# Five layer norms with the reciprocal deviations spread by two 16-bit matmuls, written out by half images

## Chip, cores and metric

The kernel runs on one core of one Trainium2 chip. The metric is the device time of one execution in microseconds (us). TensorE does the matmuls (PE in the profile's rows; PEld is its loading of weights), VectorE is DVE, ScalarE is ACT, GpSimd is POOL. SBUF is the on-chip memory that all of them read, PSUM the memory that matmuls write.

## The reference, cut to what matters

A feature map of 8 images, 128 channels and 32 x 32 pixels goes through a window attention, a gated depthwise convolution, and then, as 1024 tokens of 128 channels per image, through full attention, a mixture of gelu experts, a local attention and a mixture of silu experts. Every token stage begins with a layer norm over the channels, and the local attention ends with a fifth that has a gain and an offset:

```python
def _ln_t(v, eps=1e-05):
    m = jnp.mean(v, axis=-1, keepdims=True)
    s = jnp.var(v, axis=-1, keepdims=True)
    return (v - m) / jnp.sqrt(s + eps)

t = t + _L2_attn_ref(_ln_t(t), ...)
t = t + _L2_ffn_ref(_ln_t(t), ...)
t = t + _L3_attn_ref(_ln_t(t), gamma, beta)   # ends with (out - mu) * rsqrt(var + EPS) * gamma + beta
t = t + _L3_ffn_ref(_ln_t(t), ...)
```

## The kernel before

The whole network is one program of stages, one behind the other; each stage ends with a barrier of all engines (`Chip.stage`, L68 to L76). `network` calls `layer_norm` (L1425) five times: ahead of the token attention (L2300), ahead of the gelu experts (L2313, weights are fetched meanwhile), ahead of the local attention (L2317), behind it (L2321, the one with gain and offset, called the fourth below), and ahead of the silu experts (L2329, again with a fetch). Nothing else runs in these stages.

The map X lies in SBUF with the 128 channels on the partitions, so a mean over channels is a sum over partitions, which TensorE makes. The work is cut into 16 halves of images, 512 tokens each. For a half there are these steps, all in float32 unless said otherwise:

- mean (L1465, TensorE): one matmul with a matrix whose entries are 1/128 leaves the mean of each token on all partitions, 128 x 512 in PSUM (`m_ps`);
- centre (L1513, VectorE): `xc` = X minus `m_ps`;
- Square (L1495, ScalarE): `sq`;
- variance (L1473, TensorE): four matmuls with `sq` as weights and one column of 1/128, so that the 512 variances come out as a tile of 128 x 4 (`v_ps`), tokens on the partitions;
- Sqrt (L1500, ScalarE) and reciprocal (L1519, VectorE), both on 128 x 4: `sd` and `rs`;
- broadcast (L1483, TensorE): four matmuls of 128 x 128 with a column of `rs`, repeated, as weights and the unit matrix as data put each token's reciprocal deviation back on all partitions, 128 x 512 in PSUM (`r_ps`);
- finish: XN = `xc` times `r_ps` (L1523, VectorE), or in the fourth norm t = `xc` times gamma times `r_ps` (L1526) and X = t + beta + X (L1530).

The order on each engine is written out by hand in pairs of halves (an image), in a hardware loop that `periods` (L1446) makes: the front of an image (two means, two centres) stands ahead of the back of the image before it (on VectorE two reciprocals and two finishes, on TensorE two variances and two broadcasts). Semaphores tie the engines together. GpSimd has no instruction in these stages.

Of the kernel before, what the change touches and what calls it, by code (L numbers as in the profile page):

```python
# [47 lines left out]
LO = 2.0 ** 11  # L48
# [1376 lines left out]
def layer_norm(chip, src, mean_w, eps5, identf, dst=None, X=None, gamma=None, beta=None, fetch=None):  # L1425

    nc = chip.nc
    TILES = HALF // C
    with chip.stage() as ctx:
        xc = chip.buf(ctx, "xc", [C, 2, 2, HALF])
        sq, t = (chip.buf(ctx, n, [C, 2, HALF]) for n in ("sq", "t"))
        sd, rs = (chip.buf(ctx, n, [C, 2, TILES]) for n in ("sd", "rs"))
        scratch = chip.buf(ctx, "scratch", [1, 8])
        m_ps, v_ps, r_ps = (chip.psum(ctx, n, [C, 2, HALF]) for n in ("m_ps", "v_ps", "r_ps"))
        mean_ready, centred, squared, var_ready, rooted, inverted, spread, scaled, stored = (chip.sem(s) for s in (
            "mean_ready", "centred", "squared", "var_ready", "rooted", "inverted", "spread", "scaled", "stored"))  # L1440

        def periods(engine, front, back):


            front(0, 0)
            with engine.Fori(0, B // 2 - 1) as i:  # L1446
                for odd in (1, 0):
                    front(i * 2 + (2 - odd), odd)
                    back(i * 2 + (1 - odd), 1 - odd)
            front(B - 1, 1)  # L1450
            back(B - 2, 0)
            back(B - 1, 1)

        with nc.Block() as block:
            if fetch is not None:
                @block.sync
                def _(sp):
                    fetch.load(sp)

            @block.tensor  # L1460
            def _(pe):
                def front(i, odd):
                    for c in range(2):
                        pe.wait_ge(centred, i * 2 + c + 1)
                        nc.tensor.matmul(m_ps[:, c], mean_w[:], src[:, i, c * HALF:(c + 1) * HALF],  # L1465
                                         start=True, stop=True).then_inc(mean_ready, 1)

                def middle(i):
                    for c in range(2):
                        pe.wait_ge(squared, i * 2 + c + 1)  # L1470
                        pe.wait_ge(rooted, i * 2 + c + 1)
                        for n in range(TILES):
                            mm = nc.tensor.matmul(v_ps[:, c, n:n + 1], sq[:, c, n * C:(n + 1) * C], mean_w[:, 0:1],  # L1473
                                                  start=True, stop=True)
                        mm.then_inc(var_ready, 1)

                def back(i, odd):
                    middle(i)
                    for c in range(2):
                        pe.wait_ge(inverted, i * 2 + c + 1)  # L1480
                        pe.wait_ge(scaled, i * 2 + c + 3)
                        for n in range(TILES):
                            mm = nc.tensor.matmul(r_ps[:, c, n * C:(n + 1) * C],  # L1483
                                                  rs[:, c, n:n + 1].to_broadcast([C, C]), identf[:], start=True, stop=True)
                        mm.then_inc(spread, 1)

                periods(pe, front, back)

            @block.scalar
            def _(act):  # L1490
                def front(i, odd):
                    for c in range(2):
                        act.wait_ge(centred, i * 2 + c + 3)
                        act.wait_ge(var_ready, i * 2 + c + 1)
                        nc.scalar.activation(sq[:, c], xc[:, odd, c], ACT.Square).then_inc(squared, 1)  # L1495

                def back(i, odd):
                    for c in range(2):
                        act.wait_ge(var_ready, i * 2 + c + 3)
                        nc.scalar.activation(sd[:, c], v_ps[:, c, 0:TILES], ACT.Sqrt, bias=eps5[:]).then_inc(rooted, 1)  # L1500

                with act.Fori(0, B // 2) as i:
                    for odd in range(2):
                        front(i * 2 + odd, odd)
                        back(i * 2 + odd, odd)

            @block.vector
            def _(v):
                def front(i, odd):
                    for c in range(2):  # L1510
                        v.wait_ge(mean_ready, i * 2 + c + 1)
                        v.wait_ge(scaled, i * 2 + c + 1)
                        nc.vector.tensor_tensor(xc[:, odd, c], src[:, i, c * HALF:(c + 1) * HALF], m_ps[:, c],  # L1513
                                                ALU.subtract).then_inc(centred, 1)

                def back(i, odd):
                    for c in range(2):
                        v.wait_ge(rooted, i * 2 + c + 3)
                        nc.vector.reciprocal(rs[:, c], sd[:, c]).then_inc(inverted, 1)  # L1519
                    for c in range(2):  # L1520
                        v.wait_ge(spread, i * 2 + c + 1)
                        if dst is not None:
                            nc.vector.tensor_tensor(dst[:, i, c * HALF:(c + 1) * HALF], xc[:, odd, c], r_ps[:, c],  # L1523
                                                    ALU.mult).then_inc(scaled, 1)
                            continue
                        nc.vector.scalar_tensor_tensor(t[:, c], xc[:, odd, c], gamma[:], r_ps[:, c],  # L1526
                                                       ALU.mult, ALU.mult).then_inc(scaled, 1)
                        v.wait_ge(scaled, i * 2 + c + 5)
                        at = X[:, i, c * HALF:(c + 1) * HALF]
                        nc.vector.scalar_tensor_tensor(at, t[:, c], beta[:], at, ALU.add, ALU.add).then_inc(stored, 1)  # L1530

                grant(nc, scratch, [(centred, 2), (rooted, 2), (var_ready, 2), (scaled, 4)])
                periods(v, front, back)


def token_projections(chip, XN, dram, qk_scr, v_scr):
# [586 lines left out]
def local_attention(chip, XN, dram, identf, out):  # L2123
# [131 lines left out]
def network(nc, x, dram, out):  # L2255
# [12 lines left out]
    with ExitStack() as ctx:  # L2268
# [143 lines left out]
```

## Time and profile before

| | us |
|---|---|
| median of three runs | 3694.21 |
| the three runs | 3693.68, 3694.21, 3706.76 |
| the profiled execution, its own time | 3697.97 |
| its span (first to last instruction in the trace) | 3696.2 |
| the five layer norms' stretches together | 237.6 |

Over the whole span the page has TensorE busy 88%, VectorE 74%, ScalarE 57% and GpSimd 31%; most of that is attention and experts. The norms are some 6.4% of the span, so they have to be read by themselves: by the busy times of a stretch, by the instructions in order of time, and by the mean durations of a line. A bracket at a row's end says how long the engine was idle ahead of it and what ended that. A group that repeats (x16) is given with its start and the length to its last end, which overlaps the next group's start by some 0.1 to 0.2 us on TensorE, since its ends are modelled. PEclk is the share of TensorE's full clock that was granted: 1.00 is 2.4 GHz and 0.50 is 1.2 GHz.

### The profile page before, as it was taken

The numbers are of one execution on the slowest core, as the hardware profiler recorded it, in microseconds if no ns is written. First come the engines' busy times: TensorE is split into PE (matmuls) and PEld (weight loads), VectorE is DVE, ScalarE is ACT, GpSimd is POOL, SyncE is SP. The second block draws the span as 40 slices with busy tenths as digits, with TensorE's granted clock in tenths as the row PEclk, the third lists the DMA queues.
The fourth block names the chain that finished last, engine by engine and source line by source line (L and its number), as shares of the span: only waits on it lengthen the run. The fifth ranks groups of instructions, "written<-read, shape, count | busy, mean of one in ns | idle before, by whom it ended". The sixth has DMA issues, their size and how long they took to land. (4 is left out here: it accounts for less than half of the span.)

```text
span 3696.2 us, 77563 instructions
## 1 busy us (share of the span) xinstructions
PE 3265.0 (88%) x29519; PEld 1473.0 (40%) x29519; DVE 2743.4 (74%) x4441; ACT 2106.7 (57%) x2679; POOL 1139.6 (31%) x990
## 2 busy tenths in 40 slices
PE   5978887467799999999999999779978959999999
PEld 3545554134222222222222222633466724444444
DVE  6468885564799999999999995244377467777776
ACT  2338887012277777787778778334333335555555
POOL 4515656000000000000000000034300168888887
PEclk9979999788699999999999999779988779999999
DMA  5756664003200010001000000034300133233320
GB/s 158 209 142 137 139 145 88 4 0 139 70 17 23 17 28 17 23 17 28 23 17 24 22 18 5 19 114 152 103 1 0 47 103 102 92 85 100 90 85 29
DMA packets 133923, 243.65 MB, mean 66 GB/s; under 512 B 34984, under 2 KB 47440, under 8 KB 133136
## 3 DMA queue, kind: packets, MB, share of 16 engines
q1 hardware_dynamic: 125968, 221.96, 21.5%
q0 software_dynamic: 7680, 17.84, 2.1%
q8 instruction: 195, 3.19, 0.4%
q14 instruction: 80, 0.66, 0.1%
HBM read 167.36 MB, written 56.62 MB: 61 GB/s over the span
## 5 line engine op out<-in xcount | busy, mean ns | idle before, releaser
L1170 DVE TENSOR_REDUCE mxv<-mx_ps 128x1 f32<-128x512 f32 x2048 | 1255.4, 681 | 58.2 <-PE mx_ps L1024 57.7
L1145 ACT ACTIVATE PT<-st_ps 128x1024 f32<-128x1024 f32 x1024 | 998.3, 1021 | 267.5 <-PE st_ps L1037 262.8
L1054 PE MATMUL o_ps<-PT,VA 128*32 128x256 f32 x8192 | 655.6, 392 | 3.8 <-ACT OR L1129 1.2
L2119 POOL TENSOR_TENSOR hg<-u,gb 128x512 f32<-128x512 f32 x352 | 580.4, 1654 | 130.2 <-DVE u L2080 99.9
L1024 PE MATMUL mx_ps<-KS,QS 24*128 24x512 f16 x2048 | 581.5, 393 | 35.8 <-DVE mxv L1170 19.2
L1037 PE MATMUL st_ps<-QS,KS 26*128 26x512 f16 x2048 | 398.5, 386 | 0.0
L2080 DVE TENSOR_TENSOR u<-h_ps,s 128x512 f32<-128x512 f32 x352 | 242.9, 690 | 189.3 <-ACT s L2041 185.0
L2041 ACT ACTIVATE s<-h_ps 128x512 f32<-128x512 f32 x352 | 209.9, 596 | 283.5 <-PE h_ps L1996 283.5
L720 DVE TENSOR_REDUCE mxv<-mx_ps 128x4 f32<-128x512 f32 x512 | 321.0, 682 | 44.5 <-PE mx_ps L588 40.0
L425 POOL TENSOR_TENSOR mt<-nm,less 128x16 f32<-128x16 f32 x64 | 13.8, 216 | 1066.8 <-DVE nm L1175 1066.8
L696 ACT ACTIVATE PT<-st_ps 128x1024 f32<-128x1024 f32 x256 | 262.0, 1026 | 60.4 <-PE st_ps L604 54.0
L1994 PE MATMUL h_ps<-xh,m_wh 128*128 128x512 f16 x704 | 268.2, 381 | 11.7 <-DVE xl L2063 8.9
L1995 PE MATMUL h_ps<-xl,m_wh 128*128 128x512 f16 x704 | 268.3, 381 | 0.0
L1996 PE MATMUL h_ps<-xs,m_wl 128*128 128x512 f16 x704 | 268.2, 381 | 0.0
L1054 PEld LDWEIGHTS o_ps<-PT,VA 128*32 128x32 f32 x8192 | 163.1, 108 | 240.7 <-issue 230.1
L2069 DVE TENSOR_TENSOR hl<-hg,hh 128x512 f16<-128x512 f32 x352 | 257.5, 732 | 0.1
L1024 PEld LDWEIGHTS mx_ps<-KS,QS 24*128 24x128 f16 x2048 | 146.7, 91 | 189.1 <-DVE mxv L1170 165.6
L1037 PEld LDWEIGHTS st_ps<-QS,KS 26*128 26x128 f16 x2048 | 96.3, 91 | 314.5 <-issue 314.5
L2036 ACT CAST hh<-hg 128x512 f16<-128x512 f32 x352 | 214.8, 610 | 4.3 <-POOL hg L2119 4.1
L430 PE MATMUL st_ps<-KS,ident 128*128 128x512 f16 x512 | 200.0, 391 | 9.4 <-ACT TX L1135 8.4
L619 PE MATMUL o_ps<-PT,VA 128*32 128x128 f32 x4096 | 175.4, 288 | 32.2 <-ACT OR L689 23.9
L588 PE MATMUL mx_ps<-QK 24*128 24x128 f16 x2048 | 135.4, 229 | 20.2 <-DVE scratch L58 15.2
(276 smaller groups left out, 4860.8 us busy)
## 6 DMA issues: line engine op xcount, KB each, us to landing
gb<-g SPq DMA_DIRECT2D x64, 512.0 KB
gb<-g SPq DMA_DIRECT2D x32, 1024.0 KB, 5.6
QK<-qk SPq DMA_DIRECT2D x128, 192.0 KB
qk<-hl SPq DMA_DIRECT2D x80, 256.0 KB, 3.3
gb<-g SPq DMA_DIRECT2D x64, 192.0 KB, 5.7
qk<-hl SPq DMA_DIRECT2D x64, 128.0 KB, 3.3
v<-vs SPq DMA_DIRECT2D x32, 256.0 KB, 3.3
VS<-v POOLq DMA_DIRECT2D x32, 256.0 KB, 6.0
```

The source lines that it names most:

```text
L696: nc.scalar.activation(PT[:, n % 2, 2 * a:2 * a + 2], st_ps[:, a], ACT.Exp, scale=SCALE).then_inc(st_free[a], 1)
L720: nc.vector.tensor_reduce(mxv[:, u % 2, j, n // 2 % 2, at:at + 4], mx_ps[:, slot].rearrange("p (w k) -> p w k", w=4), AX.X, ALU.max).then_ ...
L1024: nc.tensor.matmul(mx_ps[:, use % 3, :], rows(QS, g // 2, j, STACK)[:, t * C:(t + 1) * C], rows(KS, g // 2, j, STACK)[:, half * HALF:(half ...
L1037: mm = nc.tensor.matmul(st_ps[:, a, e], rows(KS, g // 2, 2 * a + e, ROWS)[:, kt * C:(kt + 1) * C], rows(QS, g // 2, 2 * a + e, ROWS)[:, g ...
L1054: mm = nc.tensor.matmul(o_ps[32 * j:32 * j + 32, at], VA[:, g // 2 % 2, kt, j, :], PT[:, n % 2, j, at], start=(kt == 0 and half == 0), sto ...
L1145: nc.scalar.activation(PT[:, n % 2, 2 * a:2 * a + 2], st_ps[:, a], ACT.Exp, scale=1.0 / SHIFT ** 2).then_inc(st_free[a], 1)
L1170: nc.vector.tensor_reduce(mxv[:, g % 2, j, t, half:half + 1], mx_ps[:, slot], AX.X, ALU.max).then_inc(mx_free, 1)
L1994: nc.tensor.matmul(out, wh[:, m, c, :], xh[:, s], start=True, stop=False)
L1995: nc.tensor.matmul(out, wh[:, m, c, :], xl[:, s], start=False, stop=False)
L1996: mm = nc.tensor.matmul(out, wl[:, m, c, :], xs[:, s], start=False, stop=True)
L2069: nc.vector.tensor_tensor(hl[:, n % PARTS], hg[:, n % HG_SLOTS], hh[:, n % PARTS], ALU.subtract).then_inc(low_part, 1)
L2119: nc.gpsimd.tensor_tensor(hg[:, n % HG_SLOTS], u[:, n % H_SLOTS], gb[:, s, tile], ALU.mult).then_inc(gated, 1)
```

## The change

`layer_norm` is written anew; nothing outside it changes.

- The loop is gone. Each engine's program is written out over the 16 halves. TensorE and VectorE begin with two halves of means and centres; then for half u TensorE has mean(u+2), variance(u), broadcast(u-2), and VectorE centre(u+2), reciprocal(u), a cast of it, finish(u-2), diagonal tile(u).
- The broadcast is no longer four float32 matmuls with `rs` as weights. The reciprocal is split into a 16-bit part `rh` (the cast, L1530, VectorE) and the rest `rl` (L1570, GpSimd). Two 128 x 512 tiles in float16 are made from them: `dh` = unit matrix times `rh` (L1536, VectorE) and `dl` = unit matrix, scaled by 2048, times `rl` (L1574, GpSimd), four diagonal blocks each. Two 16-bit matmuls of 512 columns with all-ones weights (1, and 1/2048) add them up in `r_ps` (L1484, L1485).
- Buffers: `xc` has six halves rather than four, `m_ps` three rather than two, `sd` and `rs` four rather than two, `dh` and `dl` three.
- ScalarE makes the two unit matrices in 16 bits once for each norm (L1501, L1502), VectorE the two matrices of ones (L1552, L1553).

```diff
-                        for n in range(TILES):
-                            mm = nc.tensor.matmul(r_ps[:, c, n * C:(n + 1) * C],
-                                                  rs[:, c, n:n + 1].to_broadcast([C, C]), identf[:], start=True, stop=True)
-                        mm.then_inc(spread, 1)
+                def mean(u):
+                    if u >= 3:
+                        pe.wait_ge(centred, u - 2)
...
+                def variance(u):
+                    pe.wait_ge(squared, u + 1)
+                    if u >= 2:
+                        pe.wait_ge(rooted, u - 1)
...
+                def broadcast(u):
...
+                    pe.wait_ge(diag_h, u + 1)
+                    pe.wait_ge(diag_l, u + 1)
+                    if u >= 2:
+                        pe.wait_ge(scaled, u - 1)
+                    nc.tensor.matmul(r_ps[:, u % 2], ones_h[:], dh[:, u % 3].rearrange("p n c -> p (n c)"), start=True, stop=False)
+                    nc.tensor.matmul(r_ps[:, u % 2], ones_l[:], dl[:, u % 3].rearrange("p n c -> p (n c)"),
+                                     start=False, stop=True).then_inc(spread, 1)
...
+                def invert(u):
+                    v.wait_ge(rooted, u + 1)
+                    if u >= 4:
+                        v.wait_ge(rested, u - 3)
+                    nc.vector.reciprocal(rs[:, u % 4], sd[:, u % 4]).then_inc(inverted, 1)
+                    v.wait_ge(inverted, u + 1)
+                    nc.vector.tensor_copy(rh[:, u % 4], rs[:, u % 4]).then_inc(rounded, 1)
+
+                def diag(u):
+                    v.wait_ge(rounded, u + 1)
+                    if u >= 3:
+                        v.wait_ge(spread, u - 2)
+                    nc.vector.tensor_tensor(dh[:, u % 3], *diagonal(id_h, rh[:, u % 4]), ALU.mult).then_inc(diag_h, 1)
...
+                for u in range(UNITS):
+                    if u + AHEAD < UNITS:
+                        centre(u + AHEAD)
+                    invert(u)
+                    if u >= LAG:
+                        finish(u - LAG)
+                    diag(u)
...
+            @block.gpsimd
+            def _(pool):
+                pool.wait_ge(ready, 4)
+                for u in range(UNITS):
+                    pool.wait_ge(rounded, u + 1)
+                    nc.gpsimd.tensor_tensor(rl[:, u % 4], rs[:, u % 4], rh[:, u % 4], ALU.subtract).then_inc(rested, 1)
+                    pool.wait_ge(rested, u + 1)
+                    if u >= 3:
+                        pool.wait_ge(spread, u - 2)
+                    nc.gpsimd.tensor_tensor(dl[:, u % 3], *diagonal(id_l, rl[:, u % 4]), ALU.mult).then_inc(diag_l, 1)
```

`diagonal` repeats the unit matrix over four blocks and each of the four columns over its block.

VectorE in the loop of the first norm before, for one image (a row is line, operation, out<-in and shape; REGISTER_ALU rows are addresses and counts):

```order
L1513 TENSOR_TENSOR xc<-X,m_ps 128x512
L1511 REGISTER_ALU
L1513 ISA
L1513 TENSOR_TENSOR xc<-X,m_ps 128x512
L1518 ISA
L1519 RECIPROCAL rs<-sd 128x4
L1518 REGISTER_ALU
L1519 RECIPROCAL rs<-sd 128x4
L1521 REGISTER_ALU
L1523 ISA
L1523 TENSOR_TENSOR XN<-xc,r_ps 128x512
```

VectorE in the first norm now, for two halves from the third on:

```order
L1522 TENSOR_TENSOR xc<-X,m_ps 128x512
L1528 RECIPROCAL rs<-sd 128x4
L1530 CAST rh<-rs 128x4
L1541 TENSOR_TENSOR XN<-xc,r_ps 128x512
L1536 TENSOR_TENSOR dh<-id_h,rh 128x512
L1522 TENSOR_TENSOR xc<-X,m_ps 128x512
L1528 RECIPROCAL rs<-sd 128x4
L1530 CAST rh<-rs 128x4
L1541 TENSOR_TENSOR XN<-xc,r_ps 128x512
L1536 TENSOR_TENSOR dh<-id_h,rh 128x512
```

A cast and a tile of 128 x 512 came onto VectorE for each half, and one finish now stands between the cast and that tile. In the fourth norm the place of the finish holds two instructions (names as above, O is the local attention's output):

```order
L1522 TENSOR_TENSOR xc<-O,m_ps 128x512
L1528 RECIPROCAL rs<-sd 128x4
L1530 CAST rh<-rs 128x4
L1545 SCALAR_TENSOR_TENSOR t<-xc,gamma,r_ps 128x512
L1548 SCALAR_TENSOR_TENSOR X<-t,beta,X 128x512
L1536 TENSOR_TENSOR dh<-id_h,rh 128x512
```

There both instructions of the finish come ahead of the diagonal tile. GpSimd in a norm now, where it had no row before, for three halves:

```order
L1570 TENSOR_TENSOR rl<-rs,rh 128x4
L1574 TENSOR_TENSOR dl<-id_l,rl 128x512
L1570 TENSOR_TENSOR rl<-rs,rh 128x4
L1574 TENSOR_TENSOR dl<-id_l,rl 128x512
L1570 TENSOR_TENSOR rl<-rs,rh 128x4
L1574 TENSOR_TENSOR dl<-id_l,rl 128x512
```

Each pair begins when VectorE's cast of that half is done, so it runs beside the finish and the diagonal tile on VectorE.

## Rows read from the trace of the kernel before

**Rows 1.** Busy us of each engine by stretch: four norms and expert work; then PEclk.
```profile
808.90:854.40 45.50, 44.66 (x288) 35.33 (x288) 24.97 (x52) 13.17 (x32) 0.00 (x0) 0.96 0.00 0
2332.30:2378.80 46.50, 45.58 (x288) 35.72 (x288) 24.97 (x52) 23.33 (x40) 0.00 (x0) 0.93 0.07 23
...
2825.50:2879.70 54.20, 50.45 (x288) 39.39 (x288) 36.14 (x68) 23.31 (x40) 0.00 (x0) 0.86 0.00 0
2880.40:2925.60 45.20, 44.28 (x288) 35.16 (x288) 24.97 (x52) 13.15 (x32) 0.00 (x0) 0.96 0.24 96
3100.00:3600.00 500.00, 500.00 (x2318) 226.23 (x2317) 369.37 (x539) 295.01 (x539) 425.20 (x258) 1.00 0.31 91
```

**Rows 2.** Instructions in order of time in the first norm: start, duration (us), engine, line.
```profile
821.59 2.03 PE L1483 MATMUL r_ps<-identf,rs 128*128 128x128 f32 x16
...
823.46 1.88 PE L1465 MATMUL m_ps<-X,mean_w 128*128 x4
...
825.17 1.84 PE L1473 MATMUL v_ps<-mean_w,sq 128*128 128x1 f32 x16
...
826.16 0.26 ACT L1500 ACTIVATE sd<-v_ps,eps 128x4 f32<-128x4 f32 x1 [2.84 <-PE v_ps L1473]
...
826.88 2.03 PE L1483 MATMUL r_ps<-identf,rs 128*128 128x128 f32 x16
```

**Rows 3.** VectorE by line and shape: count, busy us, mean ns, idle before.
```profile
L1519 DVE RECIPROCAL rs<-sd 128x4 f32<-128x4 f32 x80 | 14.0, 177 | 36.7 <-ACT sd L1500 36.2
...
L1530 DVE SCALAR_TENSOR_TENSOR X<-t,beta,X 128x512 f32 x12 | 9.0, 751 | 1.6
...
L1755 DVE TENSOR_TENSOR M<-M,prefer 128x512 f32<-128x512 f32 x2 | 1.4, 692 | 0.1
```

**Rows 4.** GpSimd by line and shape, the same columns.
```profile
L425 POOL TENSOR_TENSOR VA<-VS,unit 128x512 f32<-128x512 f32 x32 | 33.4, 1045 | 13.4 <-DVE VA L716 9.4 <-PE o_ps L619 2.7
L425 POOL TENSOR_TENSOR xph<-xh,unit 128x1024 f16<-128x1024 f16 x8 | 15.3, 1918 | 0.0
...
L425 POOL TENSOR_TENSOR mt<-nm,less 128x16 f32<-128x16 f32 x64 | 13.8, 216 | 1066.8 <-DVE nm L1175 1066.8
```

**Rows 5.** GpSimd in order of time, in the gelu experts.
```profile
2467.09 1.26 POOL L1884 TENSOR_TENSOR hg<-hs,gb 128x512 f32<-128x512 f32 x1 [1.86 <-ACT hs L1870]
```

**Rows 6.** VectorE and GpSimd in order of time, in the last router.
```profile
2957.33 5.21 POOL L425 TENSOR_TENSOR m_wl<-w_full,lift 128x2816 f16<-128x2816 f32 x1
...
2959.89 3.19 DVE L1742 TENSOR_TENSOR P<-P,r 128x512 f32<-128x512 f32 x1
2962.50 5.95 POOL L1666 TENSOR_TENSOR w_full<-w_full,m_wh 128x2816 f32<-128x2816 f32 x1
...
2963.84 5.16 DVE L1746 TENSOR_TENSOR M<-P,m 128x512 f32<-128x512 f32 x1
2968.53 5.21 POOL L425 TENSOR_TENSOR m_wl<-w_full,lift 128x2816 f16<-128x2816 f32 x1
```

**Rows 7.** VectorE and GpSimd in order of time, in the silu experts (h_ps in PSUM).
```profile
3299.31 0.69 DVE L2080 TENSOR_TENSOR u<-h_ps,s 128x512 f32<-128x512 f32 x1 [0.65 <-ACT s L2041]
...
3299.92 0.68 DVE L2069 TENSOR_TENSOR hl<-hg,hh 128x512 f16<-128x512 f32 x1
...
3300.08 1.65 POOL L2119 TENSOR_TENSOR hg<-u,gb 128x512 f32<-128x512 f32 x1 [0.30 <-DVE u L2080]
...
3301.25 0.69 DVE L2080 TENSOR_TENSOR u<-h_ps,s 128x512 f32<-128x512 f32 x1 [0.66 <-ACT s L2041]
```

**Rows 8.** The fourth norm in order of time: its start, and TensorE at 2838 to 2844.
```profile
2825.60 5.85 PE L1465 MATMUL m_ps<-O,mean_w 128*128 128x512 f32 x8 [3.10 <-DVE scratch L58]
...
2830.74 0.69 DVE L1513 TENSOR_TENSOR xc<-O,m_ps 128x512 f32<-128x512 f32 x1 [0.63 <-PE m_ps L1465]
...
2838.77 2.50 PE L1483 MATMUL r_ps<-identf,rs 128*128 128x128 f32 x16 [0.35 <-DVE rs L1519]
...
2838.85 1.28 ACT L1495 ACT_TABLE_LOAD   x1
...
2841.06 3.15 PE L1465 MATMUL m_ps<-O,mean_w 128*128 x4
```

**Rows 9.** Busy times and PEclk in a stretch of the fourth norm, columns as above.
```profile
2840.50:2843.50 3.00, 3.00 (x7) 1.57 (x7) 2.75 (x5) 2.08 (x3) 0.00 (x0) 0.50 0.00 0
```

More of the change, by code:

```diff
@@ L1432, in layer_norm, with half, diagonal @@
     TILES = HALF // C
+    UNITS, AHEAD, LAG, KEPT = 2 * B, 2, 2, 6
+    def half(buf, u):
+        return buf[:, u // 2, u % 2 * HALF:(u % 2 + 1) * HALF]
     with chip.stage() as ctx:
-        xc = chip.buf(ctx, "xc", [C, 2, 2, HALF])
+        ones_h, ones_l, id_h, id_l = (chip.buf(ctx, n, [C, C], F16) for n in ("ones_h", "ones_l", "id_h", "id_l"))
+        xc = chip.buf(ctx, "xc", [C, KEPT, HALF])
         sq, t = (chip.buf(ctx, n, [C, 2, HALF]) for n in ("sq", "t"))
[L1436 to L1452, printed above, removed]
+        sd, rs, rl = (chip.buf(ctx, n, [C, 4, TILES]) for n in ("sd", "rs", "rl"))
+        rh = chip.buf(ctx, "rh", [C, 4, TILES], F16)
+        dh, dl = (chip.buf(ctx, n, [C, 3, TILES, C], F16) for n in ("dh", "dl"))
+        m_ps = chip.psum(ctx, "m_ps", [C, 3, HALF])
+        v_ps, r_ps = (chip.psum(ctx, n, [C, 2, HALF]) for n in ("v_ps", "r_ps"))
+        mean_ready, centred, squared, var_ready, rooted, inverted, rounded, rested, spread, scaled, stored = (
+            chip.sem(s) for s in ("mean_ready", "centred", "squared", "var_ready", "rooted", "inverted", "rounded", "rested",
+                                  "spread", "scaled", "stored"))
+        ready, diag_h, diag_l = (chip.sem(s) for s in ("ready", "diag_h", "diag_l"))
+        def diagonal(ident, column):
+            return ident[:].unsqueeze(1).to_broadcast([C, TILES, C]), column.unsqueeze(2).to_broadcast([C, TILES, C])
         with nc.Block() as block:
@@ L1461, in _ @@
             def _(pe):
[L1462 to L1471, printed above, removed]
-                        for n in range(TILES):
-                            mm = nc.tensor.matmul(v_ps[:, c, n:n + 1], sq[:, c, n * C:(n + 1) * C], mean_w[:, 0:1],
-                                                  start=True, stop=True)
-                        mm.then_inc(var_ready, 1)
@@ L1477, in back @@
[L1477 to L1482, printed above, removed]
-                            mm = nc.tensor.matmul(r_ps[:, c, n * C:(n + 1) * C],
-                                                  rs[:, c, n:n + 1].to_broadcast([C, C]), identf[:], start=True, stop=True)
-                        mm.then_inc(spread, 1)
@@ L1487, in _ @@
-                periods(pe, front, back)
+                def mean(u):
+                    if u >= 3:
+                        pe.wait_ge(centred, u - 2)
+                    nc.tensor.matmul(m_ps[:, u % 3], mean_w[:], half(src, u), start=True, stop=True).then_inc(mean_ready, 1)
+                def variance(u):
+                    pe.wait_ge(squared, u + 1)
+                    if u >= 2:
+                        pe.wait_ge(rooted, u - 1)
+                    for n in range(TILES):
+                        mm = nc.tensor.matmul(v_ps[:, u % 2, n:n + 1], sq[:, u % 2, n * C:(n + 1) * C], mean_w[:, 0:1],
+                                              start=True, stop=True)
+                    mm.then_inc(var_ready, 1)
@@ new lines, in broadcast @@
+                def broadcast(u):
+                    if u == 0:
+                        pe.wait_ge(ready, 4)
+                    pe.wait_ge(diag_h, u + 1)
[5 more added lines that the diff above has]
+                                     start=False, stop=True).then_inc(spread, 1)
@@ L1489, in _ @@
+                for u in range(AHEAD):
+                    mean(u)
+                for u in range(UNITS):
+                    if u + AHEAD < UNITS:
+                        mean(u + AHEAD)
+                    variance(u)
+                    if u >= LAG:
+                        broadcast(u - LAG)
+                for u in range(UNITS - LAG, UNITS):
+                    broadcast(u)
             @block.scalar
             def _(act):
[L1491 to L1505, printed above, removed]
+                nc.scalar.copy(id_h[:], identf[:]).then_inc(ready, 1)
@@ new lines, in _ @@
+                nc.scalar.activation(id_l[:], identf[:], ACT.Copy, scale=LO).then_inc(ready, 1)
+                for u in range(UNITS + 1):
+                    if u < UNITS:
+                        act.wait_ge(centred, u + 1)
+                        if u >= 2:
+                            act.wait_ge(var_ready, u - 1)
+                        nc.scalar.activation(sq[:, u % 2], xc[:, u % KEPT], ACT.Square).then_inc(squared, 1)
+                    if u:
+                        act.wait_ge(var_ready, u)
+                        if u > 4:
+                            act.wait_ge(inverted, u - 4)
+                        nc.scalar.activation(sd[:, (u - 1) % 4], v_ps[:, (u - 1) % 2, 0:TILES], ACT.Sqrt,
+                                             bias=eps5[:]).then_inc(rooted, 1)
@@ L1507, in _ @@
             @block.vector
             def _(v):
[L1509 to L1530, printed above, removed]
@@ L1532, in _, with centre @@
-                grant(nc, scratch, [(centred, 2), (rooted, 2), (var_ready, 2), (scaled, 4)])
-                periods(v, front, back)
+                def centre(u):
+                    v.wait_ge(mean_ready, u + 1)
+                    if u >= KEPT:
+                        v.wait_ge(scaled, u - KEPT + 1)
+                    nc.vector.tensor_tensor(xc[:, u % KEPT], half(src, u), m_ps[:, u % 3], ALU.subtract).then_inc(centred, 1)
+                def invert(u):
[5 more added lines that the diff above has]
+                    nc.vector.tensor_copy(rh[:, u % 4], rs[:, u % 4]).then_inc(rounded, 1)
@@ new lines, in diag, with finish @@
+                def diag(u):
[3 more added lines that the diff above has]
+                    nc.vector.tensor_tensor(dh[:, u % 3], *diagonal(id_h, rh[:, u % 4]), ALU.mult).then_inc(diag_h, 1)
+                def finish(u):
+                    v.wait_ge(spread, u + 1)
+                    if dst is not None:
+                        nc.vector.tensor_tensor(half(dst, u), xc[:, u % KEPT], r_ps[:, u % 2], ALU.mult).then_inc(scaled, 1)
+                        return
+                    if u >= 2:
+                        v.wait_ge(stored, u - 1)
+                    nc.vector.scalar_tensor_tensor(t[:, u % 2], xc[:, u % KEPT], gamma[:], r_ps[:, u % 2],
+                                                   ALU.mult, ALU.mult).then_inc(scaled, 1)
+                    v.wait_ge(scaled, u + 1)
+                    nc.vector.scalar_tensor_tensor(half(X, u), t[:, u % 2], beta[:], half(X, u), ALU.add, ALU.add).then_inc(stored, 1)
@@ new lines, in _ @@
+                for u in range(AHEAD):
+                    centre(u)
+                nc.vector.memset(ones_h[:], 1.0).then_inc(ready, 1)
+                nc.vector.memset(ones_l[:], 1 / LO).then_inc(ready, 1)
+                v.wait_ge(ready, 4)
+                for u in range(UNITS):
+                    if u + AHEAD < UNITS:
+                        centre(u + AHEAD)
+                    invert(u)
+                    if u >= LAG:
+                        finish(u - LAG)
+                    diag(u)
@@ new lines, in _ @@
+                for u in range(UNITS - LAG, UNITS):
+                    finish(u)
+            @block.gpsimd
+            def _(pool):
+                pool.wait_ge(ready, 4)
+                for u in range(UNITS):
+                    pool.wait_ge(rounded, u + 1)
[4 more added lines that the diff above has]
+                    nc.gpsimd.tensor_tensor(dl[:, u % 3], *diagonal(id_l, rl[:, u % 4]), ALU.mult).then_inc(diag_l, 1)
```

## The prediction, made before the changed kernel ran

> **What bounds the kernel now.** First the busy times of each norm's stretch [rows 1]. In the first norm TensorE is busy 44.66 of 45.50 us, VectorE 24.97, ScalarE 13.17, GpSimd not at all. The four norms without gain take 45.2 to 46.5 us. The fourth takes 54.2, with TensorE at 50.45 and a mean clock of 0.86 rather than 0.93 to 0.96.
>
> Then the order of time in the first norm [rows 2]. The broadcast begins at 821.59, the mean at 823.46, the variance at 825.17, the next broadcast at 826.88. For an image that is 1.87 + 1.71 + 1.71 = 5.29 us, with no gap. So TensorE sets the pace, 2.645 us for a half: 0.935 broadcast, 0.855 mean, 0.855 variance. In the fourth norm other things show too: TensorE waits 0.35 us ahead of the broadcast at 2838.77, ScalarE loads a table for 1.28 us at 2838.85 [rows 8], and the clock falls to 0.50 [rows 9].
>
> **What the change takes from TensorE.** 500 us of expert work hold 2318 matmuls back to back at full clock, 16-bit with 512 columns: 0.216 us each [rows 1]. Two of them are 0.43 us in place of 0.935. TensorE's work for a half falls to 0.855 + 0.855 + 0.43 = 2.14 us. If it stayed the bound, that would be 0.505 x 80 = 40 us less. It doesn't stay the bound.
>
> **What it puts on VectorE.** In a half VectorE has centre 0.69 and finish 0.69 (the product with one operand in PSUM, as the u at 3299.31 [rows 7]), reciprocal 0.18 [rows 3], the cast, which I price like the reciprocal (0.18, same 128 x 4), and the tile `dh`. No row shows a 16-bit product of two operands in SBUF; the nearest is M at 0.692 in 32 bits [rows 3]. Instructions back to back overlap by 0.08 (u starts at 3299.31, hl at 3299.92, 0.61 later for 0.69 of duration [rows 7]), except where one waits for the one ahead, as the cast does. The sum is 0.61 + 0.10 + 0.21 + 0.61 + 0.61 = 2.14 and a little for links: 2.15 to 2.45. By itself VectorE would thus be level with TensorE.
>
> **What GpSimd does to it.** In the router GpSimd and VectorE work on SBUF at the same time. P at 2959.89 takes 3.19 us and ends at 2963.08; GpSimd's instruction ahead of it ended at 2957.33 + 5.21 = 2962.54. M at 2963.84 ends at 2969.00; GpSimd's ended at 2962.50 + 5.95 = 2968.45 [rows 6]. The same form takes 0.69 alone [rows 3]. So a VectorE instruction with two operands in SBUF that comes while GpSimd works is held, and ends 0.54 to 0.55 us after GpSimd's end. One with an operand in PSUM is not: the u at 3301.25 takes 0.69 inside GpSimd's 3300.08 to 3301.73 [rows 7].
>
> Now the order after the change. The end of cast(u) releases GpSimd, 0.08 later (u ends at 3300.00, hg starts at 3300.08 [rows 7]). `rl` takes about 0.22 by the 128 x 16 form [rows 4], then again 0.08, so `dl` starts at 0.38. VectorE meanwhile does finish(u-2), not held, and comes to `dh` at 0.61. `dl` is under way, so `dh` is held. The margin is about 0.2 us.
>
> `dl` itself: 1.05 as the 128 x 512 product with a repeated operand; half of the 16-bit 128 x 1024 one is 0.96 [rows 4]; the product of two full operands is 1.26 [rows 5]. I take 1.05, nearest in size and form. It ends at 0.38 + 1.05 = 1.43 and `dh` at 1.43 + 0.545 = 1.97. Then centre(u+2) adds 0.61, reciprocal 0.10, cast 0.21: the next cast ends at 2.89. With 0.96 that is 2.80, with 1.26 it is 3.10. If `dh` ran in 0.27 after its release, half of 0.545, the period would be 2.6. **So I take 2.88 us for a half, VectorE and GpSimd in a ring, against 2.645 before.** TensorE then waits 0.74 in each.
>
> **One norm.** The third mean of the fourth norm is read at 2830.74, so it was done 5.0 us after the first began at 2825.60 [rows 8]; it starts at low clock in all. After the change three means stand first as well: 5.0, a variance 0.86, Sqrt with reciprocal and cast and their links 0.8, so the first cast ends at 6.7. The next three casts come at TensorE's pace, 1.71 + 1.71 + 2.14 = 5.6, since it has no broadcast at first. Ten more follow at 2.88 = 28.8, the last two without a centre at 2.27 = 4.5. Then `dh` ends after 1.97, the two matmuls take 0.43, with links 0.3, and the last product 0.69: 3.4. Sum 49.0 us. From the first mean to the last product the four took about 45.4, 46.3, 46.0 and 45.0 before (the stretches less some 0.1 to 0.2 of edges). That is 4 x 49.0 - 182.7 = **+13.3 us**.
>
> **The fourth norm.** Here the finish holds two instructions, and the second (X, 0.75 [rows 3]) reads t and X, both in SBUF: it arrives at 0.75 while `dl` runs, is held to 1.97, then `dh` 0.61, centre 0.61, reciprocal and cast 0.31: 3.5 us for a half. It has the same start, 6.7; two gaps of 1.7; eleven of 3.5 = 38.5; two of 2.9 without a centre = 5.8; an end of 4.9. Sum 59.3 against 54.0: **+5.3 us**. The table loads, one in each turn of the loop before [rows 8], become one for a norm, which lies in the start beside the means; they cost nothing now since the ring is longer than ScalarE's 0.9 us for a half.
>
> **The clock.** In the fourth norm the granted clock fell to 0.50 after TensorE had waited 0.35 us and done one-column matmuls ahead of that; four mean matmuls took 3.15 instead of 1.88 there [rows 2, 8, 9]. Now TensorE waits 0.74 of 2.88 us in four norms and 1.36 of 3.5 in the fourth, more than there. I put in one fall for each norm: a stretch of 3 us at half rate [rows 9] costs 1.5 us of TensorE's work, of which the waits hide some: 1.2 each, **+6 us** for five; bounds 0 and, if it stays low, the rival below.
>
> **The rest.** Two unit matrices and two matrices of ones are made while the first means run; they wait for nothing and nothing waits for them before the first broadcast. SyncE's fetches in two norms keep their place. Outside the norms nothing moves.
>
> Sum: +13.3 + 5.3 + 6 = +25 us on the profiled execution's 3697.97, that is 3723; on the median, 3.8 lower, **3719 us**.
>
> **Rivals.**
> - **The ring doesn't form.** If GpSimd starts `dl` 0.25 us later than I have it, `dh` comes first and GpSimd is the one that waits. The pace is then VectorE's own, 2.15 to 2.45 for a half. A norm takes 6.7 + 5.6 + 10 x 2.3 + 2 x 1.7 + 2 = 40.7, 4.8 less than before; in the fourth X is held at most a little, 54 to 59. Total -17 and, with the clock, up to 0: 3677 to 3694. For it: the margin of 0.2 us. Against it: each link in it is read from a row, and `rl` on four elements should be shorter than on sixteen. Chance 0.13.
> - **`dh` runs at twice the rate** and ends 0.27 after its release. Then 2.6 for a half, 46 for a norm, 53 to 56 for the fourth, with the clock +3 to +8: about 3700. No row has a 16-bit product from SBUF, so neither is excluded. Chance 0.10. The Trainium skill, "VectorE: DVE Perf Modes", section "What auto-detection actually checks", has the doubled rate where every tensor is 16-bit with step 1 or -1. `dh` is 16-bit in all three, but one operand, the column, is repeated with step 0 along its block; by that rule this rival doesn't occur, and no run here shows it yet.
> - **The clock falls and stays.** At 0.50 the mean takes 1.71 for a half (four in 3.15 less overlap [rows 8]), the broadcast 0.86, the variance between 0.86 and 1.71, since no row shows it at that level: 3.4 to 4.3 for a half, and TensorE is the bound again. Over some ten halves of a norm that is +5 to +14, for five norms +27 to +70 on top of the +19 of the ring: 3740 to 3783. For it: TensorE has less work in each half than the fourth norm had where it fell. Against it: the fourth norm before fell and came back, with a mean clock of 0.86 over its 54 us [rows 1]. Chance 0.17.
> - **TensorE stays the bound at 2.14:** -40 us, 3654. It needs neither VectorE's extra 0.8 nor the hold. Chance 0.02.
>
> **How the numbers follow.** The ring with brief falls of the clock has 0.55; its own range is 3703 to 3740, from 2.80 and no fall (4 x 48 + 58.5 - 236.7 = +14) to 3.10 with six falls (+45). The remaining 0.03 is for what I have not thought of. The range that should hold 8 in 10 takes in the upper half of the rival without a ring and most of the one with a low clock: 3682 to 3772. What this kernel's measurement can tell from no change is about 0.5%, 18.5 us. Faster by more (under 3676): 0.02, a good half of the 0.13, and a little of the unknown: 0.11. Within 0.5% (3676 to 3713): the rest of that rival, the doubled rate, and the third of the ring's range that lies under 3713: 0.29. Slower by more: 0.60.
>
> **What would show it.** In the norms after, `dh` should take 1.2 to 1.4 us and end some 0.54 after `dl`'s end; `dl` about 1.05, starting 0.38 after the cast; casts 2.9 apart; the two broadcast matmuls 0.43; TensorE's stretches with waits of 0.7 for a half; XN still 0.69. In the fourth norm X should take over 1.2 rather than 0.75. Norms of 48 to 50 and 59 to 62 us. It is wrong if `dh` shows 0.7 or less with `dl` stretched, or if PEclk stays at 0.5 over a norm.

## Result: slower by 0.8%, and the profile after

The changed kernel takes 3725.01 us in the median of four runs (3718.82 to 3729.08), the kernel before 3695.51 us (four runs, 3693.68 to 3706.76). The ratio is 1.0076, with a 95% interval of 1.0057 to 1.0095. So the median moved by 29.5 us. The profiled execution took 3721.75 us, with a span of 3719.9, which is 23.7 us over the span before; the executions of one kernel differ by some 10 us.

First again the busy times of the norms' stretches, the five of them this time (columns: stretch, length, busy us and instructions of PE, PEld, DVE, ACT, POOL, then PEclk, DMA share and GB/s), the answer to [rows 1]:

```profile
810.60:860.40 49.80, 40.62 (x192) 24.84 (x192) 44.88 (x82) 13.54 (x34) 20.75 (x32) 0.88 0.00 1
2339.50:2390.10 50.60, 41.28 (x192) 24.91 (x192) 44.84 (x82) 14.76 (x35) 20.75 (x32) 0.87 0.06 22
2678.00:2728.00 50.00, 41.21 (x192) 24.72 (x192) 44.61 (x82) 14.65 (x35) 20.73 (x32) 0.88 0.00 1
2840.00:2900.10 60.10, 42.54 (x192) 25.48 (x192) 54.29 (x98) 14.75 (x35) 20.73 (x32) 0.84 0.00 1
2900.70:2950.30 49.60, 42.30 (x192) 26.01 (x192) 44.11 (x81) 13.54 (x34) 20.74 (x32) 0.84 0.22 88
```

TensorE, which was busy 44.66 of 45.50 us in the first norm, is now busy 40.62 of 49.80 there, and VectorE 44.88 instead of 24.97 (time in which an instruction is held counts as busy). (The last row's stretch stops 1.1 us short of its norm's end.) The bound has changed engines. From the first mean to the end of the last product the five norms took 45.4, 46.3, 46.0, 54.0 and 45.0 us before and take 49.6, 50.4, 50.2, 59.9 and 50.6 now: 236.7 against 260.6, +23.9 us. The rest of the span is 3459.5 before and 3459.3 after, so the norms hold the whole difference.

Next, the order of time in the first norm, in one half of the steady part, the answer to [rows 2, 7] (start, duration, engine, line, what ended the wait ahead):

```profile
823.45 0.17 DVE L1530 CAST rh<-rs 128x4 f16<-128x4 f32 x1
823.53 0.68 DVE L1541 TENSOR_TENSOR XN<-xc,r_ps 128x512 f32<-128x512 f32 x1
...
823.70 0.20 POOL L1570 TENSOR_TENSOR rl<-rs,rh 128x4 f32<-128x4 f32 x1 [1.52 <-DVE rh L1530]
...
823.98 1.04 POOL L1574 TENSOR_TENSOR dl<-id_l,rl 128x512 f16<-128x512 f16 x1
...
824.13 1.44 DVE L1536 TENSOR_TENSOR dh<-id_h,rh 128x512 f16<-128x512 f16 x1
...
825.49 0.68 DVE L1522 TENSOR_TENSOR xc<-X,m_ps 128x512 f32<-128x512 f32 x1
...
826.09 0.17 DVE L1528 RECIPROCAL rs<-sd 128x4 f32<-128x4 f32 x1
...
826.28 0.17 DVE L1530 CAST rh<-rs 128x4 f16<-128x4 f32 x1
```

From cast to cast it is 2.83 us, and so in almost every half of the steady part of the four norms. `dl` starts 0.36 after the cast's end and runs from 823.98 to 825.02. `dh` comes 0.15 after `dl`, takes 1.44 and ends at 825.57, 0.55 after `dl`'s end, as the held instructions in [rows 6] did. At the start of the norm the same tile can be seen free, since VectorE had no finish to do and reached it before GpSimd got to `dl`; there `rl` is the one that is held:

```profile
816.96 0.69 DVE L1536 TENSOR_TENSOR dh<-id_h,rh 128x512 f16<-128x512 f16 x1
...
817.08 0.64 POOL L1570 TENSOR_TENSOR rl<-rs,rh 128x4 f32<-128x4 f32 x1 [157.89 <-DVE rh L1530]
```

The groups by line say the same for all 80 halves, beside [rows 3, 4] (count, busy us, mean ns, idle before):

```profile
L1536 DVE TENSOR_TENSOR dh<-id_h,rh 128x512 f16<-128x512 f16 x80 | 97.0, 1212 | 0.3
L1574 POOL TENSOR_TENSOR dl<-id_l,rl 128x512 f16<-128x512 f16 x80 | 83.1, 1039 | 6.4 <-POOL rl L1570 0.2
L1548 DVE SCALAR_TENSOR_TENSOR X<-t,beta,X 128x512 f32<-128x512 f32 x16 | 19.0, 1188 | 0.6
```

In 70 places in the trace `dh` (56) or X (14) begins while `dl` runs, and each ends 0.54 to 0.55 us after `dl`'s end; the 24 `dh` that touch no `dl` take 0.68 to 0.69. X in the fourth norm went from 751 to 1188 ns. In that norm, in order of time, X is held to 0.55 after `dl`'s end (2865.24 + 1.04 = 2866.28; X ends at 2866.83), and `dh` comes behind it, free:

```profile
2865.24 1.04 POOL L1574 TENSOR_TENSOR dl<-id_l,rl 128x512 f16<-128x512 f16 x1
...
2865.58 1.25 DVE L1548 SCALAR_TENSOR_TENSOR X<-t,beta,X 128x512 f32<-128x512 f32 x1
...
2866.75 0.68 DVE L1536 TENSOR_TENSOR dh<-id_h,rh 128x512 f16<-128x512 f16 x1
```

### The profile page after: what moved, and what is told of

Its sections match the earlier page's. It is cut to its first block and busy times, and to the rows that moved or that the text cites. A ratio compares the mean times of both kernels' runs of the same rounds, so it can differ in the third digit from the quotient of the medians.

```text
span 3719.9 us, 76499 instructions
## 1 busy us (share of the span) xinstructions
PE 3245.3 (87%) x29039; PEld 1417.1 (38%) x29039; DVE 2844.3 (76%) x4591; ACT 2082.0 (56%) x2668; POOL 1243.2 (33%) x1150
## 5 line engine op out<-in xcount | busy, mean ns | idle before, releaser
L1570 POOL TENSOR_TENSOR rl<-rs,rh 128x4 f32<-128x4 f32 x80 | 20.6, 258 | 412.8 <-DVE rh L1530 408.7
```

## Experiments

All times and ratios are against the kernel before on the same chip. "Pace" is the time from one half to the next in the steady part, "norms" the sum of the five from first mean to the end of the last product, "rest" the span without them; these come from the one profiled execution of each kernel. The rest differs by up to 5.5 us between kernels though no edit touches it, so kernels that lie close are better compared by their norms than by their times.

| kernel | pace, four norms | pace, fourth | norms | rest | ratio, 95% interval |
|---|---|---|---|---|---|
| before | 2.645 | 2.95 | 236.7 | 3459.5 | 1 |
| changed | 2.83 | 3.43 | 260.6 | 3459.3 | 1.0076 (1.0057 to 1.0095) |
| tile ahead of the finish | 2.21 | 3.34 | 228.7 | 3458.6 | 0.998 (0.997 to 0.999) |
| dl on ScalarE | 2.10 | 2.93 | 213.5 | 3454.0 | 0.993 (0.9907 to 0.9953) |
| dh on ScalarE | 2.10 | 2.83 | 209.5 | 3457.4 | 0.9944 (0.9925 to 0.9964) |
| dl twice | 2.84 | 4.28 | 289.5 | 3454.6 | 1.015 (1.0129 to 1.017) |
| old broadcast, new order | 2.645 | 2.65 | 230.1 | 3459.0 | 0.9983 (0.9973 to 0.9992) |
| dh on ScalarE, t in PSUM | 2.10 | 2.34 | 202.7 | 3459.2 | 0.9926 (0.9909 to 0.9942) |
| idle matmuls added | 2.83 | 3.43 | 255.5 | 3455.3 | one run: 3712.59 us |

### The tile ahead of the finish

Two theories stood against each other: the tile is held by GpSimd, or it costs 1.4 us by itself.

```diff
                     invert(u)
+                    diag(u)
                     if u >= LAG:
                         finish(u - LAG)
-                    diag(u)
```

> The changed kernel with one line moved: VectorE makes the diagonal tile dh ahead of the finish instead of behind it. Ring theory (GpSimd's dl starts first and holds dh, which takes 1.44 us instead of 0.69): dh now comes 0.03 us after the cast, ahead of dl, so it takes 0.69 and GpSimd's little rl is the one that is held, to about 0.65. VectorE's own work, 0.61 + 0.61 + 0.61 + 0.10 + 0.21 = 2.14 us, sets the pace: 2.15 to 2.25 for a half instead of 2.83, norms of 42 to 43 us instead of 50; in the fourth X is still held and a half takes about 3.2 instead of 3.43. Time about 3690 us, ratio to the kernel before 0.997 to 1.000. Rival, the price of the tile: dh takes 1.44 by its own (a repeated column is slow in 16 bits), with GpSimd beside it by chance: the order changes nothing, 2.8 for a half, about 3722 us, ratio 1.007.

Measured: 3688.06 us. The groups by line:

```profile
L1570 POOL TENSOR_TENSOR rl<-rs,rh 128x4 f32<-128x4 f32 x80 | 55.5, 694 | 351.3 <-DVE rh L1530 349.4
L1536 DVE TENSOR_TENSOR dh<-id_h,rh 128x512 f16<-128x512 f16 x80 | 55.4, 692 | 3.0 <-DVE rh L1530 0.3
...
L1548 DVE SCALAR_TENSOR_TENSOR X<-t,beta,X 128x512 f32<-128x512 f32 x16 | 15.9, 993 | 0.6
```

The same instructions in another order: `dh` takes 0.692 in place of 1.212 us, and the little `rl` 0.694 in place of 0.258, because it is now the second to come. The pace is 2.21, the norms are 32 us shorter. That the tile is dear by itself is refuted. In the fourth norm X is still held, 0.99, and the pace there fell by 0.09 only (3.34, a little over the 3.2 expected).

### The low part on ScalarE, then the high part

```diff
                         nc.scalar.activation(sd[:, (u - 1) % 4], ..., ACT.Sqrt, bias=eps5[:]).then_inc(rooted, 1)
+                    if u >= LAG:
+                        w = u - LAG
+                        act.wait_ge(rested, w + 1)
...
+                        for n in range(TILES):
+                            d = nc.scalar.activation(dl[:, w % 3, n], id_l[:], ACT.Copy, scale=rl[:, w % 4, n:n + 1])
+                        d.then_inc(diag_l, 1)
...
-                    nc.gpsimd.tensor_tensor(dl[:, u % 3], *diagonal(id_l, rl[:, u % 4]), ALU.mult).then_inc(diag_l, 1)
```

> The changed kernel with dl made by ScalarE (four products of 128 x 128 with a column of rl as scale) instead of GpSimd, which keeps rl alone. ScalarE has 0.9 us of work for a half and gets some 0.9 more. Ring theory: with nothing long on GpSimd dh takes 0.69 and X in the fourth norm 0.75; VectorE sets the pace at 2.15 to 2.25 for a half, 2.95 in the fourth; norms of 42 to 43 and 52 to 53 us; time about 3687 us, ratio 0.996 to 0.999. Rival, the price of the tile: dh stays at 1.2 to 1.4 us, 2.8 for a half, about 3722 us, ratio 1.007.

Measured: 3669.94 us, better than expected; some 5 us of it lie in the rest of the span, which the edit doesn't touch. The groups by line: with GpSimd left only `rl`, nothing on VectorE is held.

```profile
L1544 DVE TENSOR_TENSOR dh<-id_h,rh 128x512 f16<-128x512 f16 x80 | 54.7, 684 | 0.3
...
L1556 DVE SCALAR_TENSOR_TENSOR X<-t,beta,X 128x512 f32<-128x512 f32 x16 | 12.0, 752 | 0.6
```

In order of time the first norm shows TensorE without a gap again, broadcast at 820.86, mean at 821.29, variance at 822.15, the next broadcast at 822.96:

```profile
820.86 0.38 PE L1484 MATMUL r_ps<-dh,ones_h 128*128 128x512 f16 x1
...
821.08 0.38 PE L1485 MATMUL r_ps<-dl,ones_l 128*128 128x512 f16 x1
...
821.29 1.02 PE L1466 MATMUL m_ps<-X,mean_w 128*128 128x512 f32 x2
...
822.15 0.95 PE L1473 MATMUL v_ps<-mean_w,sq 128*128 128x1 f32 x8
...
822.96 0.38 PE L1484 MATMUL r_ps<-dh,ones_h 128*128 128x512 f16 x1
```

So 2.10 us for a half: 0.43 + 0.86 + 0.81. My expectation had VectorE at 2.15 to 2.25 as the bound; it needs no more than TensorE (in the first halves of this norm it works without a gap, and a half takes 2.08). This is the gain of the 16-bit broadcast, 0.54 us for a half, which the changed kernel didn't get.

The other way round, `dh` on ScalarE and `dl` left on GpSimd:

```diff
+                        act.wait_ge(inverted, w + 1)
...
+                            d = nc.scalar.activation(dh[:, w % 3, n], id_h[:], ACT.Copy, scale=rs[:, w % 4, n:n + 1])
+                        d.then_inc(diag_h, 1)
...
-                    diag(u)
```

> The changed kernel with dh made by ScalarE (four products of 128 x 128 with a column of the reciprocal as scale) instead of VectorE; dl stays on GpSimd. Ring theory: GpSimd's dl holds nothing on VectorE in four norms, VectorE has 1.55 us for a half, GpSimd 1.4, ScalarE 1.8, so TensorE sets the pace again at 2.14 us; norms of 40 to 42 us; in the fourth X is held to 1.97 after the cast and a half takes about 2.85, 50 to 52 us. Time about 3680 us, ratio 0.994 to 0.998. Rival, GpSimd as the bound by itself (its chain from cast to dl too long, whatever VectorE does): a half stays at 2.8, about 3722 us.

Measured: 3674.2 us. GpSimd does the same work as in the changed kernel, 1.04 us of `dl` for a half, and the four norms run at TensorE's pace of 2.10. The group of `dl` and that of X, and between them one `dl` in the first norm with a centre that lies wholly inside it and, with an operand in PSUM, isn't held:

```profile
L1575 POOL TENSOR_TENSOR dl<-id_l,rl 128x512 f16<-128x512 f16 x80 | 83.1, 1039 | 6.4 <-POOL rl L1571 0.2
...
822.48 1.04 POOL L1575 TENSOR_TENSOR dl<-id_l,rl 128x512 f16<-128x512 f16 x1
...
822.76 0.69 DVE L1530 TENSOR_TENSOR xc<-X,m_ps 128x512 f32<-128x512 f32 x1
...
L1550 DVE SCALAR_TENSOR_TENSOR X<-t,beta,X 128x512 f32<-128x512 f32 x16 | 19.0, 1188 | 0.6
```

GpSimd is no bound by itself; what cost the time was that an instruction with two operands in SBUF came on VectorE during `dl`. In the fourth norm there is one left, X at 1188 ns, and the pace is 2.83 as expected.

### The low part twice

```diff
+                    nc.gpsimd.tensor_tensor(dl[:, u % 3], *diagonal(id_l, rl[:, u % 4]), ALU.mult).then_inc(once, 1)
+                    pool.wait_ge(once, u + 1)
                     nc.gpsimd.tensor_tensor(dl[:, u % 3], *diagonal(id_l, rl[:, u % 4]), ALU.mult).then_inc(diag_l, 1)
```

> The changed kernel with GpSimd making dl twice, one after the other, into the same tile. GpSimd's own work for a half grows from 1.3 to 2.45 us, still under the 2.83 of a half. Ring theory: the second dl too lies between the cast and dh, or begins just as dh would run: a half takes 1.04 + 0.08 more, 3.9 to 4.0 us instead of 2.83; over some 13 halves in five norms +73 us: about 3798 us, ratio 1.025 to 1.030. If dh slips in between the two, then the second dl is held by dh and only part of it is seen: +0.1 to +0.6 for a half, 3730 to 3765 us. Rival, GpSimd beside the path: no change, about 3725 us, ratio 1.008.

Measured: 3749.48 us. The plain sum of +73 us was wrong, and so was no change. In the four norms the pace settled at 2.84 (2.87 in the third), hardly more than 2.83, for another reason than I had in mind (in order of time, first norm, VectorE and GpSimd):

```profile
830.36 1.04 POOL L1574 TENSOR_TENSOR dl<-id_l,rl 128x512 f16<-128x512 f16 x1
...
830.95 0.48 DVE L1530 CAST rh<-rs 128x4 f16<-128x4 f32 x1
...
831.34 0.67 DVE L1541 TENSOR_TENSOR XN<-xc,r_ps 128x512 f32<-128x512 f32 x1
...
831.48 1.04 POOL L1576 TENSOR_TENSOR dl<-id_l,rl 128x512 f16<-128x512 f16 x1
...
831.94 1.13 DVE L1536 TENSOR_TENSOR dh<-id_h,rh 128x512 f16<-128x512 f16 x1
...
832.48 0.65 POOL L1570 TENSOR_TENSOR rl<-rs,rh 128x4 f32<-128x4 f32 x1
...
833.20 1.04 POOL L1574 TENSOR_TENSOR dl<-id_l,rl 128x512 f16<-128x512 f16 x1
```

GpSimd now has no gap: `rl`, held by `dh` to 0.65, and two `dl` of 1.04, with 0.07 and 0.08 between them and an overlap of 0.04 in the records at the end, are 2.84 us. GpSimd runs half a turn late, so that the first `dl` lies beside the centre, which has an operand in PSUM and isn't held. Only the little cast is, for 0.3 us. The two engines found a phase in which most of the added 1.1 us is hidden. The 29 us that it still costs come from the longer start and end of each norm, the first halves of the third norm (4.08) and the fourth norm, where X is held by the first `dl` and `dh` by the second: 4.28 for a half, 71.6 us. The run shows that GpSimd's time is on the path, but also that a hold's price can't be added up from durations alone: it depends on which phase the engines settle in.

### The old broadcast in the new order

```diff
-                    nc.tensor.matmul(r_ps[:, u % 2], ones_h[:], dh[:, u % 3].rearrange("p n c -> p (n c)"), start=True, stop=False)
-                    nc.tensor.matmul(r_ps[:, u % 2], ones_l[:], dl[:, u % 3].rearrange("p n c -> p (n c)"),
-                                     start=False, stop=True).then_inc(spread, 1)
+                    for n in range(TILES):
+                        mm = nc.tensor.matmul(r_ps[:, u % 2, n * C:(n + 1) * C],
+                                              rs[:, u % 4, n:n + 1].to_broadcast([C, C]), identf[:], start=True, stop=True)
+                    mm.then_inc(spread, 1)
```

The cast, both tiles and GpSimd's part go too.

> The new order by half images with two halves of lag, written out, but the broadcast as before: four float32 matmuls on the reciprocals, no cast, no diagonal tiles, nothing on GpSimd. It separates the order from the diagonal tiles. If the tiles alone cost the time: TensorE sets the pace at 2.645 us for a half as before, the four norms take 44 to 46 us; the fourth loses its table loads in each turn and goes from 54 to 45 to 47; time 3684 to 3690 us, ratio 0.997 to 0.999. Rival, the order costs too (first halves, longer end): norms of 48 us and more, ratio 1.000 or above.

Measured: 3687.78 us. Four norms as before within 0.9 us, 45.4, 46.5, 45.2 and 45.2; the fourth 47.8 instead of 54.0. The busy times of the fourth, against [rows 1], show TensorE busy almost throughout, a clock of 0.95 instead of 0.86, and ScalarE with one table load (33 instructions) instead of eight (40):

```profile
2823.40:2871.40 48.00, 45.34 (x288) 35.76 (x288) 35.48 (x64) 15.24 (x33) 0.00 (x0) 0.95 0.00 1
```

So the rest of the rewrite (the order by half images, the loop written out, the deeper buffers; no run separates them) is worth 6.6 us, nearly all of it in the fourth norm, and the diagonal tiles with their cast, as the changed kernel makes them, cost 260.6 - 230.1 = 30.5 us.

### t in PSUM

The kernel with `dh` on ScalarE, and one more edit, to ask whether the hold goes by operands or by engine:

```diff
-        sq, t = (chip.buf(ctx, n, [C, 2, HALF]) for n in ("sq", "t"))
+        sq = chip.buf(ctx, "sq", [C, 2, HALF])
+        t = chip.psum(ctx, "t", [C, 1, HALF])
```

With it t has one buffer instead of two, so each t waits for the X of the half before.

> The kernel with dh on ScalarE, and in the fourth norm t in PSUM instead of SBUF, so that X = t + beta + X has one operand in SBUF only. By the theory that GpSimd holds an instruction with two operands in SBUF and no other: X takes 0.75 instead of 1.19 us, the fourth norm's half falls from 2.83 to 2.3 (VectorE: 0.61 + 0.10 + 0.21 + 0.70 + 0.70), the norm from 50 to 43 us; the four others stay at 2.10 for a half and 40 us. Time 7 us under the kernel with dh on ScalarE: 3666 us, ratio 0.991 to 0.994. Rival, the hold goes by engine and not by operands: X stays at 1.19 and the norm at 50 us.

Measured: 3665.54 us, 0.9926 of before. X is back at 0.751 beside the same `dl` on GpSimd, the fourth norm's pace 2.34 and its length 44.3 instead of 50.1:

```profile
L1551 DVE SCALAR_TENSOR_TENSOR X<-t,beta,X 128x512 f32<-128x512 f32 x16 | 12.0, 751 | 0.6
```

The hold goes by the operands: 14 of the 16 X begin while `dl` runs, and all 16 take 0.75. The "and no other" of the theory doesn't hold, as the cast in the run with `dl` twice has shown. This is the fastest of the kernels here, 27 us under the kernel before on its chip; its norms are 58 us shorter than those of the changed kernel.

### Idle matmuls

The prediction had 6 us for falls of the clock. TensorE got work that nobody reads, in its waits ahead of the broadcast:

```diff
+                def filler(times):
+                    for _ in range(times):
+                        nc.tensor.matmul(fill[:, 0], ones_h[:], id_h[:].unsqueeze(1).to_broadcast([C, TILES, C]), start=True, stop=True)
...
+                    else:
+                        filler(2 if u < UNITS - 4 else 4)
```

> The changed kernel with TensorE doing two idle 16-bit matmuls of 512 columns ahead of each broadcast, four in the last halves, into a bank that nobody reads. In the changed kernel the granted clock was 1.00 through the middle of each norm and 0.50 in its last 2 to 4 halves. If that fall costs what I put in for the clock (1.2 us for a norm), norms of 48.4 to 49.2 us in place of 49.6 to 50.6. If TensorE's waits hide it, norms within 0.4 us of before and 2.83 for a half; the two matmuls ahead of a broadcast may even delay it, by up to 0.2 us at the end of a norm.

Measured: pace 2.83 and 3.43, unchanged; norms of 49.1, 49.9, 49.5, 59.9 and 47.1 us, 5.1 less in all. First the changed kernel's clock at the end of the first norm, then this kernel's:

```profile
846.00:850.00 4.00, 2.82 (x17) 1.62 (x15) 3.93 (x10) 1.56 (x4) 1.87 (x4) 1.00 0.00 0
850.00:854.00 4.00, 2.82 (x17) 2.25 (x16) 3.97 (x7) 0.78 (x2) 1.84 (x3) 0.76 0.00 0
854.00:858.00 4.00, 2.25 (x6) 0.43 (x6) 3.93 (x8) 0.26 (x1) 2.47 (x4) 0.50 0.00 0
```

```profile
842.50:846.50 4.00, 3.54 (x24) 2.23 (x24) 3.96 (x7) 1.05 (x3) 1.84 (x3) 1.00 0.02 4
846.50:850.50 4.00, 3.16 (x14) 1.09 (x12) 3.93 (x8) 0.00 (x0) 2.48 (x4) 1.00 0.00 0
```

In the changed kernel the level was 1.00 through the middle and fell to 0.50 when the means had run out; there it costs 0.43 us at the end of each of the four norms (3.76 against 3.33 from the last cast to the end of the last product), and nothing in the fourth. The larger piece is where I hadn't looked: the fifth norm follows the fourth without other work between, and its first means ran at the level that the fourth left behind. First the changed kernel, then the one with idle matmuls:

```profile
2900.84 5.46 PE L1466 MATMUL m_ps<-X,mean_w 128*128 128x512 f32 x6 [2.61 <-PEq L75]
```

```profile
2893.64 2.81 PE L1467 MATMUL m_ps<-X,mean_w 128*128 128x512 f32 x6 [2.88 <-PEq L75]
```

The same three means, six records, 5.46 against 2.81 us; the norm's first cast ends 7.31 us after the first mean in the one and 4.31 in the other. The single time of 3712.59 is lower by more than the 5.1 us; the rest of the span differs by 4 us there, as it does between the other kernels, and is not part of the reading.

## Why the prediction was right, step by step

The forecast was 3719, the median came at 3725, and the profiled execution moved by +23.8 us where the sum said +25. The mechanism is the one that was forecast; that the sum came so close is in part luck, as the last points show.

- **TensorE's new load, 2.14 us for a half:** 2.10, measured where TensorE is the bound again (`dl` or `dh` on ScalarE).
- **VectorE's own work, 2.15 to 2.45:** 2.21 with the tile ahead of the finish, where it follows the cast that it waits for; 2.08 in the order of the change, with `dl` on ScalarE. So it is level with TensorE's, as said.
- **The hold:** `dl` was put at 0.38 after the cast and starts at 0.36; its 1.05 us are 1.04; `dh` ends 0.55 after it. The margin that decided, about 0.2 us, was 0.15 in the trace, because the finish starts some 0.08 ahead of the cast's end. The order experiment puts `dh` on the other side of it, and the kernel is then faster than before, by 0.2%. One reading was loose: the u at 3301.25, given as inside GpSimd's instruction, ends 0.21 after it. The centre inside `dl` with `dh` on ScalarE shows the point cleanly.
- **The ring's pace, 2.88:** 2.83. `dh` ends 1.95 after the cast's end where I had 1.97, and centre, reciprocal and cast add 0.88 where I had 0.92.
- **One norm, 49.0:** 49.6 in the first. The start was 6.2 rather than 6.7 there, and 7.0 to 7.3 in the others. The gap between the third and fourth cast is 3.15 where I had 2.14: the hold begins with the first finish, one half earlier than I counted, and the third cast is itself held by the `dl` before it (0.48 instead of 0.17 us), which the sum didn't have. The end is 3.8 instead of 3.4, by the low clock. The cast and the `dl` that holds it:

```profile
819.73 1.04 POOL L1574 TENSOR_TENSOR dl<-id_l,rl 128x512 f16<-128x512 f16 x1
...
820.30 0.48 DVE L1530 CAST rh<-rs 128x4 f16<-128x4 f32 x1
```

- **The fourth norm, 59.3 and 3.5 for a half:** 59.9 and 3.43.
- **The clock, +6:** near in size, wrong in place. I expected a fall within each norm, from its waits of 0.74 us in a half; in the steady parts there was none: with waits of about 0.7 us in every steady half the level stayed at 1.00, and in the fourth norm too, with waits of 1.3 us in 3.43. What the idle matmuls gave back, 5.1 us, lay at the ends of norms (4 x 0.43) and in the start of the fifth norm (3.0) and of the third (0.3). Part of that the kernel before pays too: in its fifth norm the third centre begins 4.7 us after the first mean (2880.49 to 2885.18), in the changed kernel 5.6 (2900.84 to 2906.42). So as an addition the clock was over-sized: 4 x 0.43 for the ends and 0.9 for that start make some 2.6 us. That each norm before began at low clock was misread too: the third began at 1.00 and fell 6.6 us later.
- **The sum:** without some 2.6 us of clock the norms grew by 21.3 us where the terms of the ring, 13.3 + 5.3, made 18.6. The hold that began early, 1.0 us in each of the four norms, was missing, and the pace was taken 0.05 too long. The clock, put in 3.4 too high, made up for it.
- **The range of the ring:** its lower end doesn't follow from its working. 3694 + 14 is 3708, not 3703. The measured time lies inside either way.
- **The rivals:** the ring formed. The kernel with the tile ahead of the finish is the first rival made by hand: 3688 us, inside its 3677 to 3694, with norms of 42 to 43 us rather than 40.7. The tile at double rate didn't occur: free of GpSimd it takes 0.69, as in 32 bits. That agrees with the Trainium skill, "VectorE: DVE Perf Modes", section "What auto-detection actually checks", by whose rule a tensor that is repeated with step 0 excludes the doubled rate; whether the step is the reason, no run here shows. The clock stayed low in no norm.

## What to carry to other kernels

Before a product of two SBUF operands goes onto VectorE, look in the trace for what GpSimd does at that moment: the one that comes second is held until the other has ended, so the same instructions cost 2.83 or 2.21 us for a half by their order alone. An operand in PSUM, or ScalarE with the column as its scale, takes the instruction out of the conflict. And relief on the bounding engine is worth only what the engine that takes up the work can do in the same time with its waits.

## What the runs showed of the hardware

- The hold works in both directions and on very small instructions. GpSimd's 128 x 4 subtraction takes 0.20 us free and 0.63 to 0.71 behind VectorE's `dh`.
- An instruction with one operand can be held too: with `dl` twice, the cast of 128 x 4 from 32 to 16 bits takes 0.48 us instead of 0.17 and ends at 831.43, 0.03 after `dl`'s end at 831.40. The reciprocal of the same size ahead of it, in 32 bits, takes 0.17 inside `dl`; why it isn't held, no run shows.
- Four ScalarE products of 128 x 128 with a column as scale follow each other in 1.26 us together, though each is recorded with 0.39.
- TensorE kept 1.00 of its clock with waits of about 0.7 us in every 2.83, and lost it within the last halves, without means. The fourth norm ended at 0.50, and the first means of the fifth, 0.8 us later, still ran at that level.
